# Quantised values kept as fp16 plus 1536 through their TensorE transposes, with the offset taken off by ScalarE's copy out of PSUM

## The reference

```
x = x + tanh(g_xattn[0]) * expert(layernorm(x), fside, ctx)        # two smooth-quantised int8 linears with silu(gate) * up between
x = x + tanh(g_ffn[0])   * bitffn(layernorm(x), ...)               # three bit_linear, hidden 2048
x = x + tanh(g_xattn[1]) * attention(layernorm(x), ctx, ...)       # att = softmax(q k^T) of ctx, applied to x
x = x + tanh(g_ffn[1])   * moe(layernorm(x), ...)                  # 8 experts of 16, top 2

smooth_quant_linear(x, w):  x_q = clip(round(xs / x_scale), -127, 127);  w_q = the same of ws;  x_q @ w_q.T * x_scale * w_scale.T
bit_linear(x, w, b):        x_q = clip(round(x * 127 / max|x|), -128, 127);  w_q = clip(round(w / mean|w|), -1, 1)
                            x_q @ w_q.T * (scales) + b
```

## Time and profile before

| | us |
|---|---|
| three runs | 652.31, 650.40, 647.13 |
| median | 650.4 |
| span of the profiled execution | 650.1 |
| first block | 0 to 269 |
| second block | 269 to 650, iterations of 22.03 from the third to the last but two |

### The profile page before, as it was taken

How to read it: one execution, slowest core, us unless ns; L and a number is a source line. 1 busy time by engine, 2 the same in 40 slices (tenths; PEclk the granted TensorE clock), 3 DMA queues, 4 the chain that set the end, 5 groups by cost and what they waited for, 6 DMA issues and landing times.

```text
span 650.1 us, 8671 instructions
## 1 busy us (share of the span) xinstructions
PE 513.0 (79%) x2494; PEld 255.7 (39%) x2534; DVE 500.7 (77%) x1171; ACT 330.9 (51%) x542; POOL 214.2 (33%) x292
## 2 busy tenths in 40 slices
PE   1546647845856757779999999999999999999964
PEld 1324424424533424323344344434443444344432
DVE  5697998898795789455687787878787878886743
ACT  2457638826838846544445445534543454445420
POOL 1443335445355335601232133223312330331031
PEclk9765988977978986789999999999999999999995
DMA  8964002021002500000000000000000000000000
GB/s 319 263 244 161 1 4 76 24 65 32 0 1 70 221 2 16 1 0 2 0 1 18 1 15 16 16 0 16 17 16 0 16 16 16 0 17 17 17 16 32
DMA packets 21718, 28.69 MB, mean 44 GB/s; under 512 B 8376, under 2 KB 10680, under 8 KB 21184
## 3 DMA queue, kind: packets, MB, share of 16 engines
q1 hardware_dynamic: 21696, 28.43, 13.0%
HBM read 24.15 MB, written 4.19 MB: 44 GB/s over the span
## 4 chain that ended last, share of the span: by engine, by line
PE 28%; DVE 15%; POOL 7%; ACT 5%; issue 3%; DVEq 0%; POOLq 0%
PE p_val L1641 11%; PE p_gate L1641 10%; ACT p L1581 5%; POOL ey L1387 3%; POOL rstd L159 3%; PE p_tr L1629 2%; DVE beat L1488 2%; PE p_out L1680 2%; DVE u L1416 2%; DVE mu L1418 2%; DVE stats L199 1%; DVE x_all L1439 1%; PE p_out L1647 1%; POOL rstd L158 1%; PE p_tr L1661 1%
## 5 line engine op out<-in xcount | busy, mean ns | idle before, releaser
L158 POOL TENSOR_TENSOR rstd<-mv,ln_eps 128x1 f32<-128x1 f32 x48 | 10.2, 212 | 253.6 <-DVE mv L201 253.3
L1577 ACT ACTIVATE silu_g<-p_gate,bcol 128x512 f32<-128x512 f32 x64 | 44.0, 687 | 86.5 <-PE p_gate L1641 86.5
L1416 DVE TENSOR_TENSOR u<-p_val,silu_g 128x512 f32<-128x512 f32 x64 | 44.1, 689 | 46.5 <-PE p_val L1641 44.4
L1641 PE MATMUL p_val<-val_t,q_room 128*128 128x512 bf16 x256 | 67.8, 388 | 0.0
L1641 PE MATMUL p_gate<-gate_t,q_room 128*128 128x512 bf16 x240 | 64.1, 388 | 3.2 <-PEq L371 2.3
L1680 PE MATMUL p_out<-out_t,p_t 128*128 128x512 bf16 x240 | 63.3, 384 | 3.9 <-issue 2.4
L1581 ACT ACTIVATE p<-u,bcol 128x512 f16<-128x512 f32 x64 | 42.7, 714 | 39.1 <-DVE bcol L1426 39.1
L1647 PE MATMUL p_out<-att_t,lt_c 128*128 (+1 forms) x128 | 57.7, 594 | 0.0
L1418 DVE TENSOR_REDUCE mu<-u 128x1 f32<-128x512 f32 x64 | 43.9, 686 | 2.2
L1558 ACT ACTIVATE p_t<-p_tr 128x512 bf16<-128x512 bf16 x64 | 36.3, 593 | 10.8 <-PE p_tr L1671 9.0
L1647 PEld LDWEIGHTS p_out<-att_t,lt_c 128*128 128x128 f32 x128 | 24.1, 190 | 29.6 <-issue 29.6
(11 more groups left out here) (227 smaller groups left out, 1177.5 us busy)
## 6 DMA issues: line engine op xcount, KB each, us to landing
att_t<-in_L_ffn_gate_w SPq DMA_DIRECT2D x4, 1024.0 KB, 11.4
h_region<-in_fside_BxS2xS SPq DMA_DIRECT2D x4, 1024.0 KB, 5.4
att_t<-in_L_ffn_val_w SPq DMA_DIRECT2D x4, 1024.0 KB, 8.6
out_dram<-x_all SPq DMA_DIRECT2D x16, 256.0 KB, 2.0
h_region<-in_L_ffn_out_w SPq DMA_DIRECT2D x3, 1024.0 KB, 5.7
x_all<-in_x SPq DMA_DIRECT2D x2, 1024.0 KB, 5.5
ctx_sb<-in_ctx SPq DMA_DIRECT2D x4, 512.0 KB, 3.6
x_all<-in_x SPq DMA_DIRECT2D x1, 2048.0 KB, 10.5
```

Of the source, the lines that this page charges most:

```text
L1416: nc.vector.tensor_tensor(cols, p_val[:, c % 2, :], silu_g[:, c % 2, :], ALU.mult).then_inc(u_done, 1)
L1577: nc.scalar.activation(silu_g[:, c % 2, :], p_gate[:, c % 2, :], ACT.Silu, scale=col(CG)).then_inc(silu_done, 1)
L1641: last = nc.tensor.matmul(bank[:, c % 2, :], lhs, rhs, start=k == 0, stop=k == KD)
```

## The change

Every rounded number stays fp16 plus 1536 through its transposes, with an fp16 identity `ident_16` and the PSUM bank read as fp16. ScalarE's copy out of PSUM carries a bias of -1536. The DVE passes `integers`, `q_round` and `b_round` and their semaphores are gone; PE waits for the semaphore of the ACT rounding instead. `w_ternary` is one pass: at most 1537, then at least 1535. In `q_spread` the four transposes of numbers no longer wait for the bias columns that POOL splits; the fifth one, of these columns, stays bf16, so `x_transposed` on ACT is now two instructions, over 512 and over 128 columns.

```
+        ident_16 = sb("ident_16", [P, P], F16)
+        tr_16 = [p_tr[:, r, :].bitcast(F16) for r in range(2)]
...
-        def q_round(dve, n):
-            dve.wait_ge(q_x16, n + 1)
-            need(dve, q_tr, n)
-            nc.vector.tensor_scalar(xaug[:, 0:D], x16[:, :], ROUND16, None, ALU.subtract).then_inc(q_int, 1)
...
         def x_transposed(act, n):
             act.wait_ge(q_tr, n + 1)
-            nc.scalar.activation(x_t[:, :], tr_h[1][:, 0:AUG], ACT.Copy).then_inc(xt_ready, 1)
+            nc.scalar.activation(x_t[:, 0:D], tr_16[1][:, 0:D], ACT.Copy, bias=-ROUND16)
+            nc.scalar.activation(x_t[:, D:AUG], tr_h[1][:, D:AUG], ACT.Copy).then_inc(xt_ready, 1)
...
         def q_spread(pe, n):
-            pe.wait_ge(q_int, n + 1)
+            pe.wait_ge(q_x16, n + 1)
+            for k in range(KD):
+                nc.tensor.transpose(tr_16[1][:, k * P:(k + 1) * P], x16[:, k * P:(k + 1) * P], ident_16[:, :])
             pe.wait_ge(q_parts, n + 1)
-            for k in range(KD + 1):
-                last = nc.tensor.transpose(tr_h[1][:, k * P:(k + 1) * P], xaug[:, k * P:(k + 1) * P], ident_h[:, :])
+            last = nc.tensor.transpose(tr_h[1][:, D:AUG], xaug[:, D:AUG], ident_h[:, :])
             last.then_inc(q_tr, 1)
...
-                        w_link(nc.vector.tensor_scalar(tern_slot(g), w16_slot(g), ROUND16, 1.0, ALU.subtract, ALU.min))
-                        nc.vector.tensor_scalar(tern_slot(g), tern_slot(g), -1.0, None, ALU.max).then_inc(tern_ready, 1)
+                        nc.vector.tensor_scalar(tern_slot(g), w16_slot(g), ROUND16 + 1.0, ROUND16 - 1.0, ALU.min, ALU.max).then_inc(tern_ready, 1)
...
-                    def integers(z, b, r):
-                        dve.wait_ge(a_q16[z], 2 * b + r + 1)
-                        q = q16_of[z][r]
-                        nc.vector.tensor_scalar(q.bitcast(BF16), q, ROUND16, None, ALU.subtract).then_inc(a_q[z], 1)
...
+                    def less_offset(dst, src, ready, value, done):
+                        act.wait_ge(ready, value)
+                        nc.scalar.activation(dst, src, ACT.Copy, bias=-ROUND16).then_inc(done, 1)
...
-                        pe.wait_ge(a_q[z], 2 * b + r + 1)
+                        pe.wait_ge(a_q16[z], 2 * b + r + 1)
...
-                def b_round(n, c):
-                    dve.wait_ge(b_p16, HC * n + c + 1)
-                    if c == 0:
-                        need(dve, b_tr, HC * n)
-                    cols = slice(c * 512, (c + 1) * 512)
-                    nc.vector.tensor_scalar(p_int[:, cols], p16[:, cols], ROUND16, None, ALU.subtract).then_inc(b_int, 1)
...
                 def b_spread(n, c):
-                    pe.wait_ge(b_int, HC * n + c + 1)
+                    pe.wait_ge(b_p16, HC * n + c + 1)
                     for k in range(KH // HC):
-                        last = nc.tensor.transpose(tr_h[(c + 1) % 2][:, k * P:(k + 1) * P],
-                                                   p_int[:, c * 512 + k * P:c * 512 + (k + 1) * P], ident_h[:, :])
+                        last = nc.tensor.transpose(tr_16[(c + 1) % 2][:, k * P:(k + 1) * P],
+                                                   p16[:, c * 512 + k * P:c * 512 + (k + 1) * P], ident_16[:, :])
                     last.then_inc(b_tr, 1)
```

More of the change, by code:

```diff
@@ L438, in _ @@
                 def _(pool):
-                    for mat in (ident, ident_h):
+                    for mat in (ident, ident_h, ident_16):
                         nc.gpsimd.memset(mat[:, :], 0.0).then_inc(pool_chain, 1)
-                    pool.wait_ge(pool_chain, 2)
-                    for mat in (ident, ident_h):
+                    pool.wait_ge(pool_chain, 3)
+                    for mat in (ident, ident_h, ident_16):
                         nc.gpsimd.affine_select(out=mat[:, :], in_=mat[:, :], compare_op=ALU.not_equal, fill=1.0, base=0,
@@ L529, in step @@
                         o_add(b - 1, range(2, T))
-                    pool.wait_ge(consts_made, 9)
+                    pool.wait_ge(consts_made, 10)
                     h_reciprocal_deviation(0)
@@ L913, in w_transposed @@
                                 dst, src = w_t[m][:, 8 * h:8 * h + 8, c * P:(c + 1) * P], src.rearrange("p (k n) -> p k n", k=8)
-                            copy(dst, src, tern_tr, 2 * g + h + 1, tern_copied)
+                            less_offset(dst, src, tern_tr, 2 * g + h + 1, tern_copied)
                     def smooth_rows(z, b):
@@ L934, in integers_transposed @@
                         dst = h_qT[v // 2][:, (v % 2) * 1024:(v % 2 + 1) * 1024] if z == 0 else o_qT[v][:, :]
-                        copy(dst, spread_bank[z][:, v % 2, :].bitcast(BF16), a_qT[z], QT_BANKS[z] * b + v + 1, a_qT_copied[z])
+                        less_offset(dst, spread_bank[z][:, v % 2, :].bitcast(F16), a_qT[z], QT_BANKS[z] * b + v + 1, a_qT_copied[z])
                     def scale_row(z, b):
@@ L1098, in w_transpose @@
                             need(pe, tern_copied, 2 * g + h - 1)
-                            bank = W_BANK[m][:, h, :].bitcast(BF16)
+                            bank = W_BANK[m][:, h, :].bitcast(F16)
                             for blk in range(8):
                                 at = (blk % 4) * D + (2 * h + blk // 4) * P if m < 2 else (8 * h + blk) * P
-                                last = nc.tensor.transpose(bank[:, blk * P:(blk + 1) * P], tern_slot(g)[:, at:at + P], ident_h[:, :])
+                                last = nc.tensor.transpose(bank[:, blk * P:(blk + 1) * P], tern_slot(g)[:, at:at + P], ident_16[:, :])
                             last.then_inc(tern_tr, 1)
@@ L1143, in integers @@
                             pe.wait_ge(a_rows_copied[z], (2 - z) * (b + 1))
-                        q = q16_of[z][r].bitcast(BF16)
-                        bank = spread_bank[z][:, v % 2, :].bitcast(BF16)
+                        q = q16_of[z][r]
+                        bank = spread_bank[z][:, v % 2, :].bitcast(F16)
                         for blk in range(8):
                             at = (blk % T) * width[z] + (j0 + blk // T) * P
-                            last = nc.tensor.transpose(bank[:, blk * P:(blk + 1) * P], q[:, at:at + P], ident_h[:, :])
+                            last = nc.tensor.transpose(bank[:, blk * P:(blk + 1) * P], q[:, at:at + P], ident_16[:, :])
                         last.then_inc(a_qT[z], 1)
@@ L1307, in last_step @@
                         q_spread(pe, 0)
-                    pe.wait_ge(consts_made, 9)
+                    pe.wait_ge(consts_made, 10)
                     step0()
@@ L1583, in b_transposed @@
                 def b_transposed(n, c):
-                    copy(p_t[:, c * 512:(c + 1) * 512], tr_h[(c + 1) % 2][:, 0:512], b_tr, HC * n + c + 1, pt_ready)
+                    act.wait_ge(b_tr, HC * n + c + 1)
+                    nc.scalar.activation(p_t[:, c * 512:(c + 1) * 512], tr_16[(c + 1) % 2][:, 0:512], ACT.Copy, bias=-ROUND16).then_inc(pt_ready, 1)
                 def step(i, with_c, with_d, with_e, with_q, with_q2):
```

36 lines of the change are left out of this document (10 added, 26 removed).

## The result

| | before | changed kernel |
|---|---|---|
| median of the runs | 651.36 us (4 runs, 647.13 to 652.36) | 628.33 us (4 runs, 626.46 to 628.56) |
| profiled execution, span | 650.1 us | 626.6 us |
| DVE busy | 500.7 us | 461.1 us |
| second block begins (its first matmul) | 269.05 us | 249.20 us |
| from there to the end of the span | 381.05 us | 377.4 us |

The ratio is 0.965 with an interval of 0.9613 to 0.9687, so the change gains 3.1 to 3.9%. Forecast were 632.0 us and a range of 625 to 642. The span lost 23.5 us: 19.85 in the first block (15.0 forecast) and 3.65 in the second (3.4 forecast). Single runs of the kernel before lie between 644.9 and 656.3 us over all comparisons, so single executions are compared by stretch, and only medians in total.

What follows compares the result with a forecast made beforehand. PE was taken to bound the second block, while DVE time counted in the first. Gains of 3.4 + 8.9 + 2.9 + 3.2 = 18.4 us gave 650.1 - 18.4 + 0.3 = 632.0 us, range 625 to 642.

Steps and rivals of the forecast that it cites:

- step0: First block: DVE's L652 of sample 1 starts at 78.8 instead of 87.7, 0.6 us ahead of POOL; gain 8.9 us.
- step 1: First block: shorter DVE queue and less PE waiting for removed passes; gain 1.4 us.
- step 2: First block: 0.6 + 0.6 us from the removed passes, POOL's root limiting the first part; gain 1.2 us.
- rival 2: Step 2's normalisation tile slips ahead of POOL (2.1 us), second iteration chain gives 0.3, not 0.14; 628 us, chance 0.12.
- step 3: First block: ACT is the limit in both halves, so the gain is only 0.3 us.
- last_step: First block's end: without second ternary passes `t_maximum` comes 3.2 to 4.0 us sooner; gain counted 3.2 us.
- second block: c_add released by c_attend, then a_d decides; 0.14 us in each of 13 iterations plus first and last ones; 3.4 us.
- The rival with POOL in front: Step0: POOL's 4.5 us instruction begins before DVE's L652, which starts at 83.9; 637 us, chance 0.18.
- Rivals 3 to 5: First block's gain given back, 643 (0.10); fp16 transposes at fp32 speed, 658 (0.05); ternary pass off fast rate, 646 (0.03).

Runs made afterwards that it cites:

- pool_first: Changed kernel with DVE's h_scaled_act of sample 1 waiting for POOL's scaled_weights of that sample; 633.64 us, ratio to before 0.9759.
- bias_norm: Kernel before with w_bias(1) moved right behind w_bias(0) and POOL's L505 waiting until the normalisation is over; 648.14 us, ratio 0.9965.
- ab_only: Kernel before with only the integer passes of the first block's activations and scaled weights removed; 641.68 us, ratio 0.9840.
- idle_ffn: Changed kernel with four DVE passes per second-block iteration put back, their output read by nobody; 632.58 us, ratio to before 0.9738.
- norm_free: Kernel before with POOL's L505 (o_scaled_act) waiting until DVE's normalisation is over; 647.14 us, ratio 0.9934.
- w_only: Kernel before with only the weights' part: one ternary pass, fp16 transposes, ScalarE taking off the offset; 644.96 us, ratio 0.9897.
- bias_early: Kernel before with DVE's w_bias(1) moved right behind w_bias(0), no arithmetic changed; 652.92 us, ratio 1.0015.
- adds_first: Changed kernel with all four POOL o_add placed before scaled_weights in steps 1 and 2; 623.98 us, ratio to before 0.9595.

## Why the prediction was right, and where it was off

| term | forecast | measured | |
|---|---|---|---|
| step0, start of L652/L650 of sample 1 | 8.9 | 9.56 | order as forecast; `pool_first` |
| step 1, to L650 of sample 2 | 1.4 | 0.65 | |
| step 2, to L650 of sample 3 | 1.2 | 6.41 | rival 2 came true, too |
| step 3 and last_step | 3.5 | 3.23 | |
| second block | 3.4 | 3.65 | right size, wrong next bound |

**Step0.** The order turned as worked out: the bias operation clear of POOL, L650 near 79 and ahead, POOL's row 4.94 us long, for which I had said over 5. The margin was 1.76 us instead of 0.6, since PE made the second factor row slowly at that point: four fp32 products took 3.13 us, and POOL needs both rows. With the products at the 1.98 us of before, POOL would have been ready over 1 us sooner (78.58 in `pool_first`), so by this estimate the forecast margin was about right and the wider one is luck. The rival with POOL in front would have cost the 5 us that it was priced at.

**Step 1.** The passes are worth 1.86 us here (sample 1 to 2 is 40.99 in `bias_norm` and 39.13 in `ab_only`, both with a free normalisation and a short wait; before it was 41.28). My 1.4 was too low. But the profiled execution of the changed kernel had a `t_maximum` that waited 2.17 us for PE, not 0.67, and gave 1.5 back. With the short wait it is 39.13 in `ab_only` and 39.12 in `idle_ffn`.

**Step 2.** This is the term that failed. I had the tile of 2.68 us in view and gave its release a chance of 0.12 and a price of 2.1. It was released, and was worth 3.0, since the transposes behind it ran at the higher clock too, as they did when `norm_free` released it by a wait. Another 1.5 is a wait for PE that the kernel before had in this execution and `w_only` did not. The passes gave 1.9 for 1.2. Rival 2's time, 628, is the one that came, and that is luck in part: 2.1 of its 4.2 us were to come from another iteration chain in the second block, where only 0.25 more than the forecast came. PE's wait and the clock stand in their place. The tile that was caught began at 153.1, the last of the four, 0.1 us before POOL at 153.17. The two passes in front of the normalisation were 1.2 us of DVE's queue, and half of that as a lead over POOL is enough: the distance from the normalisation's start to POOL's L505 (L504) grew from 2.48 to 3.12 us (139.33 to 142.45). It is 3.12 or 3.13 us in step 2 of all five traces without these passes. In the steps 1 and 2 of the kernels that have them and no added wait of POOL's, a tile was caught at 2.45 to 2.48 us (five times) and none at 2.54, at 3.14 and, where the normalisation itself ran 0.2 us shorter, at 2.34. So the change takes this place off the edge on which the kernel before stands. All of this stood in the trace of before, and it deserved more than 0.12.

**last_step.** `t_maximum` moved from 251.27 to 231.72. The second block began 17.48 us after it here, 17.78 before, and step 3 gave nothing by itself (0.3 us more from L650 of sample 3 to its third `t_maximum`); its forecast was 0.3, that of last_step 3.2. The second block begins at 249.20, not near 254: the 4.8 us are step 2's 5.2 with small differences. In the changed kernel the second of the two ternary passes still takes 1.53 us beside POOL:

```profile
229.66 0.69 DVE L597 TENSOR_SCALAR h_side<-h_side 128x2048 f16<-128x2048 f16 x1
230.26 1.53 DVE L597 TENSOR_SCALAR h_region<-h_region 128x2048 f16<-128x2048 f16 x1
```

**Second block.** `c_add` is released by `c_attend` as forecast. But `a_d` does not release `e_spread` after an idle PE: it ends at 448.48, and PE comes to its transpose at 448.57, straight from its own products. Next in line was PE itself. The period is 21.82 and not 21.9, as PE lost its small gaps and DVE its order-setting role together. Ten periods gave 2.2 us and the iterations around them 1.5; forecast were 1.4 and 2.0.

**Rivals 3 to 5.** Nothing was given back as a whole. fp16 transposes run like bf16 ones (221 ns mean), and the single ternary pass takes 0.68 us, so that the expensive ends of my bounds fell away.

**The rule used.** That a large POOL instruction and a two-input or two-port DVE one keep each other out for their whole length (the Trainium skill, SBUF — State Buffer, section Who interferes with whom) agrees with the rows shown here. DVE's 128 x 2048 multiplication takes 2.28 us alone and 6.58 behind POOL's 4.68, and a normalisation of four tiles 2.95 or 5.10. One row needs care: the tile that stood still for POOL began 0.06 us before POOL's instruction by the trace, so at such distances the starts in a trace don't tell who was first.

## What to carry to other kernels

When work leaves the queue of one of two engines that lock each other out, list every large operation of the other near it, and work out for each which now comes first: here such places were worth 4 to 5 us (step0) and 3 us (step 2), and the removed passes 1.9 a step. If an edit has no effect in total, look for its local gain first. `bias_early` had 4 us and lost them 16 us later to the same kind of collision. A small margin does not say by itself how safe an order is. In steps 1 and 2 POOL's multiplication began 0.24 or 0.25 us ahead of DVE's in all ten traces without `adds_first`, where both follow the same DVE passes. In step0 the order turned between traces of the same code, because slower products of PE held POOL up for 1.3 us. Where another engine feeds the two, make the order sure by a wait (`norm_free`) or a reordering (`adds_first`).

## What the runs showed that I had not expected

- The kernel before is a mixture. Of its 18 runs in the last comparison 17 lie between 644.9 and 654.2 us, those of `ab_only` between 636.9 and 642.9. One execution of `norm_free` had step0 in the other order with no edit there, through 1.1 us of a slower PE. That this makes up the whole scatter is argued, not shown.
- A lock on DVE goes along with a low clock on PE. Where PE had stood idle 3.47 us behind a blocked normalisation, sixteen fp32 transposes took 3.60 to 3.87 us instead of 2.34, with a granted clock of 0.50 from 104 to 110 us in `bias_early` and from 155 to 160 in the kernel before. Two steps without a block had the same, so the block is not the only thing that brings it.
- The length from sample 2 to sample 3 is the same to 0.02 us in the four traces without the integer passes and with POOL's old order. Differences between such rows gave the price of an event more exactly than the totals, whose runs scatter by 1%. Where the clock took another course (`bias_norm`) the sum of such prices did not hold.
